# Epilogue of finished node blocks inside the edge loop of a graph attention layer on one Trainium2 core

## What is computed

```python
h_src, h_dst = x[src], x[dst]
e = leaky_relu(concat([h_src, h_dst, ef]) @ W_attn + b_attn)
m = concat([h_src, ef]) @ W_ne
ex = exp(e - segment_max(e, dst)[dst])
z = segment_sum(ex / segment_sum(ex, dst)[dst] * m, dst)
out = relu(concat([x, z]) @ W_out)
return layernorm(x + out)
```

## Time and profile before

| | us |
|---|---|
| median of 3 runs | 4009.47 (4005.22 to 4010.96) |
| profiled execution, its time | 4021.12 |
| profiled execution, span of its trace | 4019.2 |
| busy: POOL, DVE, PE, ACT | 2972.2, 2837.8, 2260.2, 2020.9 |

### The profile page before, as it was taken

The page is one execution under the profiler, slowest core; times in us unless marked ns, Lnnn a source line. Parts: engine busy times, 40 slices in busy tenths (PEclk is TensorE's granted clock), DMA queues, the critical chain, the costliest instruction groups (busy, mean ns, idle before and its releaser), DMA issues.

```text
span 4019.2 us, 47762 instructions
## 1 busy us (share of the span) xinstructions
PE 2260.2 (56%) x9822; PEld 2005.2 (50%) x9823; DVE 2837.8 (71%) x5649; ACT 2020.9 (50%) x3433; POOL 2972.2 (74%) x3133
## 2 busy tenths in 40 slices
PE   2666655555555555555555555555555555555556
PEld 1555555544454444454444444544444544454456
DVE  8776666666766767676676766676767676766777
ACT  2665555544454444444444444444444444444446
POOL 7777777777777777777777777777777777777770
PEclk9665556556556565555655555555655556555557
DMA  6655555555555555555555555555555555555542
GB/s 166 177 173 156 159 157 156 160 158 157 158 157 157 157 157 157 157 157 157 158 157 157 157 157 157 157 158 157 157 157 157 157 157 158 157 157 157 158 147 66
DMA packets 409354, 627.14 MB, mean 156 GB/s; under 512 B 208412, under 2 KB 208796, under 8 KB 409332
## 3 DMA queue, kind: packets, MB, share of 16 engines
q1 hardware_dynamic: 296260, 519.51, 40.7%
q0 software_dynamic: 100000, 102.60, 12.3%
q10 hardware_dynamic: 13072, 4.80, 0.6%
HBM read 621.58 MB, written 4.81 MB: 156 GB/s over the span
## 4 chain that ended last, share of the span: by engine, by line
POOL 73%; issue 24%; DVE 1%; PE 1%; POOLq 1%; ACT 0%; DMA 0%; DVEq 0%
POOL V L372 73%; POOLq L390 0%; PE psE L909 0%; POOLq L381 0%; PE psT L902 0%; PE psG L844 0%; DVE y L801 0%; DVE var L782 0%; DMA V<-in_x_dram,srcs 0%; DVE y L778 0%; DVE mean L791 0%; DVE y L798 0%; DVE prod L785 0%; DMA srcs<-in_src_dram 0%; ACT zb L522 0%
## 5 line engine op out<-in xcount | busy, mean ns | idle before, releaser
L372 POOL DMA_INDIRECT V<-in_x_dram,srcs x3125 | 2971.2, 951 | 956.0 <-issue 952.9
L844 PE MATMUL psG<-V,pT 128*128 128x130 f32 x6250 | 1461.4, 427 | 366.6 <-DVE psS L663 366.6
L844 PEld LDWEIGHTS psG<-V,pT 128*128 128x128 f32 x6250 | 1361.5, 330 | 506.1 <-DVE psS L663 506.1
L837 PE MATMUL psT<-ident,e 128*128 128x128 f32 x3125 | 720.8, 404 | 1286.3 <-DVE e L658 1286.3
L448 ACT COPY pT<-psT 128x512 f32<-128x512 f32 x784 | 420.9, 589 | 1714.8 <-PE psT L837 1708.9
L837 PEld LDWEIGHTS psT<-ident,e 128*128 128x128 f32 x3125 | 573.8, 215 | 1392.7 <-DVE e L658 1392.7
L594 DVE TENSOR_TENSOR prod<-V,psM 128x512 f32<-128x512 f32 x782 | 502.4, 684 | 637.6 <-DMA V<-in_x_dram,srcs 621.8
L658 DVE TENSOR_TENSOR e<-zb,psE 128x1024 f32<-128x1024 f32 x392 | 478.8, 1221 | 259.4 <-DVE u L599 162.1
L705 DVE CUSTOM_DVE_ANT_0 um<-ubc,psS 128x1024 f32<-128x1024 f32 x391 | 477.6, 1221 | 20.2 <-ACT psS L461 19.3
L599 DVE TENSOR_REDUCE u<-prod 128x8 f32<-128x1024 f32 x391 | 477.0, 1220 | 13.5
L469 ACT ACTIVATE psE<-um,ebias 128x1024 f32<-128x1024 f32 x391 | 437.2, 1118 | 12.8
(11 more groups left out here) (97 smaller groups left out, 524.7 us busy)
## 6 DMA issues: line engine op xcount, KB each, us to landing
ubc<-scores SPq DMA_DIRECT2D x391, 512.0 KB
dbc<-in_dst_dram SPq DMA_DIRECT2D x390, 512.0 KB, 4.0
V<-in_edge_attr_dram SPq DMA_DIRECT2D x390, 256.0 KB, 2.8
V<-in_x_dram,srcs POOLq DMA_INDIRECT x3125
srcs<-in_src_dram SPq DMA_DIRECT2D x390, 4.0 KB
scores<-u SPq DMA_DIRECT2D x390, 4.0 KB
out_dram<-y SPq DMA_DIRECT2D x12, 256.0 KB
xt<-in_x_dram ACTq DMA_DIRECT2D x6, 448.0 KB, 14.2
```

What stands on the lines that cost most here:

```text
L372: nc.gpsimd.indirect_dma_start(Vx[:, s, j, 1:XW], None, x[:, :], bass.IndirectOffsetOnAxis(ap=srcs[:, s, j:j + 1], axis=0)).then_inc(h_in[ ...
L837: last = nc.tensor.transpose(psT[:, i, (j - 4 * i) * P:(j - 4 * i + 1) * P], e1[:, 0:n * P].rearrange("q (p j) -> q j p", j=n)[:, j, :], i ...
L844: last = nc.tensor.matmul(psG[:, 0:AW], pT[:, i, (j - 4 * i) * P:(j - 4 * i + 1) * P], V[:, LEADIN + s * SLOT + XW * j:LEADIN + s * SLOT + ...
```

## The change

The loop now finishes one block in every second supertile of turns 7 to 38: 160 times. In an odd supertile DVE divides a block's sums by its denominator (`prepare`), PE turns the result, ACT copies it; two supertiles on, PE multiplies it with `wz`, and in the even supertile after that DVE does the rest for a block (`finish_one`). Each five blocks share one square root on ACT at the end of the turn and one scaling on DVE in the next (`scale_group`); SP stores five blocks in the turn after. Which block is finished where is computed on the chip once behind turn 6 (`tabulate`): a block may be finished once no later supertile touches it, at most one new block for each of the 160 places; where none is new, the last one is finished and stored again. By the reference's inputs the table runs from block 0 to block 94. The last supertile runs through the windows from `ends[0]` to the last block (by these inputs one window, block 97) and finishes one block in each of them, in a longer form of the window; the last six blocks are finished together behind the last merge.

```diff
+            def store_rows(k, q):
+                m = k - YT - 2
+                at = sp.snap(blocks[q], min_val=0, max_val=NB - 3)
+                sp.wait_ge(rows_out[q - 1], 16 * (m + 3) if q else 16 * (m + 2))
+                sp.wait_ge(scaled, m + 2)
+                sp.dma_start(out[bass.ds(at * P, P), :], ro[:, q, :]).then_inc(rows_out[q], 16)
...
+            finished(TURNS + 1)
+            for q in range(GROUP):
+                store_rows(TURNS + 1, q)
+            for q in range(GROUP):
+                sp.wait_ge(rows_out[q], 16 * (TURNS - YT) + 32)
+            sp.wait_ge(back_rows, 1)
...
+                    if not ahead:
+                        act.wait_ge(z_turned, late)
+                        nc.scalar.copy(zTs[:, :], zT_ps).then_inc(z_copied, 1)
+                        act.wait_ge(scaled, late_rows)
+                        rows = act.snap(of_block, min_val=0, max_val=NB - 3)
+                        act.dma_start(out[bass.ds(rows * P, P), :], ro[:, GROUP - 1, :]).then_inc(late_out, 16)
...
+                    if not ahead:
...
+                        act.wait_ge(fin_q, late)
+                        nc.scalar.activation(fs[:, GROUP - 1:GROUP], fv[:, GROUP - 1:GROUP], ACT.Sqrt).then_inc(std_ready, 1)
...
+                    if s % 2:
+                        act.wait_ge(z_turned, GROUP * (k - YT) + s // 2 + 2)
+                        nc.scalar.copy(zTs[:, :], zT_ps).then_inc(z_copied, 1)
+                act.wait_ge(fin_q, GROUP * (k - YT) + GROUP + 1)
+                nc.scalar.activation(fs[:, 0:GROUP], fv[:, 0:GROUP], ACT.Sqrt).then_inc(std_ready, 1)
+            act.wait_ge(z_done, EVENTS + 1)
...
+            act.wait_ge(rows_out[GROUP - 1], 16 * (TURNS - YT) + 32)
             supertile(TURNS, 0, False)
...
+            def prepare(f):
+                b = bass.ds(f, 1)
+                dve.wait_ge(z_turned, fp)
+                dve.wait_ge(rescaled, settled)
+                nc.vector.tensor_scalar(fl[:, 0:1], accv[:, b, 0], TINY, None, ALU.max).then_inc(fin_l, 1)
+                dve.wait_ge(fin_l, fp)
+                nc.vector.reciprocal(fl[:, 0:1], fl[:, 0:1]).then_inc(fin_rl, 1)
+                dve.wait_ge(fin_rl, fp)
+                nc.vector.tensor_scalar(zs[:, :], accv[:, b, 1:1 + 2 * F].rearrange("p b f -> p (b f)"), fl[:, 0:1], None, ALU.mult).then_inc(zs_ready, 1)
+                dve.reg_add(fp, fp, 1)
+
+            def finish_block(f, q, product):
+                b = bass.ds(f, 1)
+                dve.wait_ge(z_done, product)
+                nc.vector.tensor_tensor(fy[:, 0:F], z_out, y0[:, b, :].rearrange("p b f -> p (b f)"), ALU.add).then_inc(fin_y, 1)
+                dve.wait_ge(fin_y, fe)
+                nc.vector.scalar_tensor_tensor(fr[:, 0:F], fy[:, 0:F], 0.0, xt[:, b, :].rearrange("p b f -> p (b f)"), ALU.max, ALU.add).then_inc(fin_r, 1)
+                dve.wait_ge(fin_r, fe)
+                nc.vector.tensor_reduce(fm[:, 0:1], fr[:, 0:F], AX, ALU.add).then_inc(fin_m, 1)
...
+                nc.vector.scalar_tensor_tensor(fout[:, q, :], fm[:, 0:1].broadcast_to((P, F)), -1.0 / F, fr[:, 0:F], ALU.mult, ALU.add).then_inc(fin_c, 1)
...
+                nc.vector.tensor_tensor(fy[:, 0:F], fout[:, q, :], fout[:, q, :], ALU.mult).then_inc(fin_s, 1)
...
+                nc.vector.tensor_reduce(fv[:, q:q + 1], fy[:, 0:F], AX, ALU.add).then_inc(fin_w, 1)
...
+                nc.vector.tensor_scalar(fv[:, q:q + 1], fv[:, q:q + 1], 1.0 / F, EPS, ALU.mult, ALU.add).then_inc(fin_q, 1)
...
+            def scale(q, n):
+                nc.vector.reciprocal(rs[:, q:q + n], fs[:, q:q + n]).then_inc(rs_ready, 1)
+                dve.wait_ge(rs_ready, fd)
+                nc.vector.tensor_tensor(ro[:, q:q + n, :], fout[:, q:q + n, :], rs[:, q:q + n].unsqueeze(2).broadcast_to((P, n, F)), ALU.mult).then_inc(scaled, 1)
...
+            def scale_group(k):
+                dve.wait_ge(std_ready, k - YT + 1)
+                for q in range(GROUP):
+                    dve.wait_ge(rows_out[q], 16 * (k - YT + 1))
+                scale(0, GROUP)
...
+                if finishing and s == 0:
+                    scale_group(k)
+                if finishing and s % 2 == 0:
+                    finish_one(k, s // 2)
+                if finishing and s % 2 == 1:
+                    prepare(dve.snap(finish[s // 2 + 2], min_val=0, max_val=NB - 3))
                 if left >= 2:
...
+            tabulate()
...
+                finished(k)
...
+            dve.sem_inc(prod_done, 1)
+            dve.wait_ge(y_copied, PAIRS + 2)
+            scale_group(TURNS)
...
+            dve.wait_ge(rows_out[GROUP - 1], 16 * (TURNS - YT) + 32)
...
             supertile(TURNS, 0, 0)
...
+            def z_step(k, q):
+                pe.wait_ge(prod_done, RING * k + 2 * q + 4)
+                pe.wait_ge(z_copied, GROUP * (k - YT) + q + 1)
+                z_multiply().then_inc(z_done, 1)
+                pe.wait_ge(zs_ready, GROUP * (k - YT) + q + 1)
+                z_turn().then_inc(z_turned, 1)
...
+                    if not ahead:
+                        pe.wait_ge(zs_ready, late)
+                        z_turn().then_inc(z_turned, 1)
+                        pe.reg_add(late, late, 1)
+                        pe.wait_ge(z_copied, late)
+                        z_multiply().then_inc(z_done, 1)
                     window(s, J if ahead else JL)
```

More of the change, by code:

```diff
@@ L321, in _, with finished @@
                 load_src(RING + s, s)
-            with sp.Fori(1, TURNS - 1) as k:
+            blocks = [sp.alloc_register(f"block_sp{q}") for q in range(GROUP)]
+            def finished(k):
+                at = GROUP * (k - YT - 2)
+                sp.load(blocks, fint[0:1, bass.ds(at, GROUP)] if not isinstance(k, int) else fint[0:1, at:at + GROUP])
+            def store_rows(k, q):
[4 more added lines that the diff above has]
+                sp.dma_start(out[bass.ds(at * P, P), :], ro[:, q, :]).then_inc(rows_out[q], 16)
+            with sp.Fori(1, YT + 2) as k:
                 for s in range(RING):
                     step(k, s)
+            sp.wait_ge(table, 1)
+            with sp.Fori(YT + 2, TURNS - 1) as k:
+                finished(k)
+                for s in range(RING):
+                    step(k, s)
+                    if 0 < s <= GROUP:
+                        store_rows(k, s - 1)
+            finished(TURNS - 1)
             for s in range(RING):
@@ L329, in _ @@
                 step(TURNS - 1, s)
+                if 0 < s <= GROUP:
+                    store_rows(TURNS - 1, s - 1)
+            finished(TURNS)
             for s in range(RING - LEAD):
@@ L499, in _ @@
             weights_out(1)
[L502 to L526, removed]
-                    nc.scalar.activation(ubc[:, par, 0:w2 * F].rearrange("p (b f) -> p b f", f=F), y0[:, bass.ds(8 * (o - 2), w2), :],
-                                         ACT.Square).then_inc(sq_ready, 1)
-            octets(octet, 3)
+            act.wait_ge(scaled, late_rows)
+            rows = act.snap(of_block, min_val=0, max_val=NB - 3)
+            act.dma_start(out[bass.ds(rows * P, P), :], ro[:, GROUP - 1, :]).then_inc(late_out, 16)
+            act.reg_add(sent, sent, 16)
+            act.wait_ge(back_turned, 1)
+            nc.scalar.copy(pT[:, 0, :], psT[:, 0, :])
+            nc.scalar.copy(pT[:, 1, 0:(BACK - 4) * P], psT[:, 1, 0:(BACK - 4) * P]).then_inc(back_copied, 1)
+            act.wait_ge(late_out, sent)
+            act.wait_ge(back_var, 1)
+            nc.scalar.activation(fs[:, :], fv[:, :], ACT.Sqrt).then_inc(back_std, 1)
         @block.vector
@@ L682, in pass_on @@
                 dve.reg_add(g, g, 1)
-            def supertile(k, s, left, y_steps=None):
+            fe = dve.alloc_register("finishing")
+            fp = dve.alloc_register("preparing")
+            finish = [dve.alloc_register(f"finish{q}") for q in range(GROUP + 2)]
+            dve.reg_mov(fe, 1)
+            dve.reg_mov(fp, 1)
+            settled = dve.alloc_register("settled")
+            fd = dve.alloc_register("scaling")
+            dve.reg_mov(fd, 1)
+            def prepare(f):
[8 more added lines that the diff above has]
+                dve.reg_add(fp, fp, 1)
@@ L685, in supertile @@
+            def supertile(k, s, left, y_steps=None, finishing=False):
                 t = RING * k + s
@@ L693, in supertile @@
                     ts = bass.ds(t, 1)
+                    if left == 0:
+                        prepare(dve.snap(of_block, min_val=0, max_val=LAST - 1))
+                        scale_late()
                     weigh()
@@ L805, in _ @@
+            nc.vector.tensor_scalar(fv[:, :], fv[:, :], 1.0 / F, EPS, ALU.mult, ALU.add).then_inc(back_var, 1)
+            dve.wait_ge(back_std, 1)
+            step(nc.vector.reciprocal(rs[:, :], fs[:, :]))
+            nc.vector.tensor_tensor(rows, rows, spread(rs), ALU.mult).then_inc(back_rows, 1)
         @block.tensor
```

270 lines of the change are left out of this document (174 added, 96 removed).

## The result

| | before | after |
|---|---|---|
| median, four runs each | 4009.43 us (4005.22 to 4010.96) | 4122.01 us (4121.49 to 4122.65) |
| ratio, 95% interval | | 1.0283 (1.0265 to 1.0300) |
| span of the profiled execution | 4019.2 us | 4119.9 us |

The forecast was 3994, the range ended at 4046. The change costs 112.6 us.

A forecast was written before the change was run, and what follows sets the result against it. POOL's gathers were taken to bound the loop, hiding 14.7 of DVE's 14.85 us added per turn. The end's -27.7 us and DVE's lag of 12.8 gave -14.9, from the median 4009.47 to 3994; range 3979 to 4046.

The forecast's parts named there:

- the start of a turn: DVE at each turn's beginning: seven more registers and a possible wait for ACT, 1.1 us more, bounds 0 to 2.
- the sum: All work added to DVE in a turn: 14.85 us against 14.7 free, with bounds of 12 to 18.
- finish_block: DVE's work for one block: six operations of 64 columns, a small one and gaps, 1.82 us.
- odd supertiles behind ACT's copy: In odd supertiles L459 and L461 queue behind ACT's copy of the turned block; just fits, cost 0, bound 0.7 each.
- scaling to the last window: five stores: At the end ACT and DVE wait for five stores, each waiting for the one before: 8.75 us, 7 to 11.5.
- last window, L730 to L730: In the last window PE turns the block only behind its eight matmuls: 12.4 us instead of 6.33.
- last merge to the end: Behind the last merge six blocks are finished together, from matmuls to stores: 13.8 us.
- the free time: DVE's waits for gathers in a turn, 17.1 us less nine gaps of 0.27: 14.7 us to hide new work in.
- the tail: The end of the span behind the last gathers: 3991.5 against 4019.2, so -27.7 us without DVE's lag, bounds 5 each way.
- DVE becomes the bound: In each turn's ten blocks, DVE work beyond 14.7 us costs 32 us per microsecond; at 1.9 over, 4050; chance 0.28.
- The pair is held for the whole operation: DVE's new operations hold up POOL's gathers for their whole length: POOL loses 17 us, time 4001; chance 0.05.
- A pause behind each table load: ACT's switches between exponential and root each pause as long as the load: 82 us beyond the forecast, 4076; chance 0.03.

## Why the prediction was wrong

**The step that failed is the start of a turn**, 1.1 us with bounds 0 and 2. It priced seven registers, and a jump back that costs what it cost before. The jump back did not stay what it was: 0.25 us in before, 3.07 in after. With the load's 1.63 that is 4.45 more, and the start measured 4.5 more instead of 1.1; besides, two operations in the turn come 0.4 late. No row of before shows such a fetch, for before never had one: the bounds were taken from rows in which the resource is not used up. The body's length, which was there to be counted, did not enter the sum, and neither did the load's own record in before: 1.37 us for twenty registers, more than the 1.1 taken for seven.

The Trainium skill has the mechanism, "Runtime: NRT & Kernel Launch", section "Instruction fetch mechanics": an engine's instruction store holds two blocks of 256 instructions, and a taken branch to a block outside of it waits for a fetch. The runs agree with the wait, and not with two blocks as what stays: the body from 104 to 478 lies in two such blocks and was fetched anew each turn. Whether the store is smaller, or keeps room for a line ahead, no run shows. By that section of the Trainium skill a load takes about 0.2 us a register, by estimate 1.4 for seven and 4 for twenty; the traces do not bear that out, with 1.63 for seven and 1.37 for twenty.

**Of the rest, term by term:**

| term | predicted | measured |
|---|---|---|
| `finish_block` | 1.82 | 1.81, and 0.4 late once a turn |
| `prepare` | 0.78 | 0.75, and 0.4 late once a turn |
| `scale_group` | 0.75 | 0.70 |
| start of a turn, more than before | 1.1 (0 to 2) | 4.5; 1.6 without the fetch |
| odd supertiles behind ACT's copy | 0 | nothing new: 14.6 us of waits for L513 in the whole span, 19.3 for L461 before |
| `tabulate`, once | 8 | 7.4 |
| scaling to the last window: five stores | 8.75 | 8.4 |
| last window, L730 to L730 | 12.4 | 12.55 |
| last merge to the end | 13.8 | 13.8 |

The operations, down to 64 columns that no row showed, came out within a tenth. So did the free time: without the fetch the sum is 13.0 + 0.75 + 1.6 = 15.35, 0.65 over the 14.7, and the ten turns from 2500 on measured 0.4 longer than before (100.79 against 100.42). Over all 32 turns, from the loop's first L730 to the third last of the span, it is 3216.9 against 3197.5, 0.6 a turn. The working has one slip: the steps up to the five stores add up to 3947.5, not 3947.7, which changes nothing.

**Two smaller errors are in the 8.7 us that are left without the fetch.** The load of registers was 0.5 too small: 32 turns make 16 us. And the tail was set against a profiled execution that was itself slow in the tail. The same epilogue, in the kernel with the load added to before and used, from its last merge on (columns as in the earlier trace rows):

```profile
3943.50:4004.10 60.60, 35.49 (x294) 33.08 (x294) 50.44 (x108) 42.91 (x150) 0.00 (x0) 0.88 0.21 54
```

The 294 matmul records take 35.5 us here and 44.8 in the earlier trace rows; the mean granted clock is 0.88 here and 0.73 there, both between the two levels of 1.2 and 2.4 GHz. From the third last `weigh` (L658 in before) to the end of the span this kernel takes 78.2 us, not 83.2. Of the five traces that have this tail, two take 83.2 (before, and the loop at 239), at a mean granted clock of 0.72, and three take 78.0 to 78.2, at 0.78 to 0.85; the two long ones are also the longest executions. So against most executions the tail wins 23, not 28: part of the 11.65 us between profiled execution and median lay in the very piece that the change removes, and was counted twice; that the tail came out as forecast is in part luck. Why some executions were granted less is open. With the first block of the loop, for which DVE waits 2.4 us once, -15 + 16 + 5 + 2.4 = +8.4; measured +8.7, which is closer than the terms are known. The fetch adds the other 104.

**The rivals.** "DVE becomes the bound" named the right engine and the right price, 32 us for each microsecond of a turn, but its worst case was 1.9 over; the turn became 4.0 longer, by a cause that it did not name. "The pair is held for the whole operation" did not show: the gathers take 946 to 950 ns in all kernels with the change, and 948 to 951 in the five without it, where the rival's 17 us would have made them 5 ns longer. By the rule of the Trainium skill, "SBUF — State Buffer", section "SBUF: two separate sides", which it states for a GpSimd operation that reads SBUF, they would have become longer; no run shows it. "A pause behind each table load" did not show either. ACT's timeline at the start of a turn of the changed kernel:

```profile
2720.92 1.28 ACT L565 ACT_TABLE_LOAD   x1
2722.21 0.21 ACT L565 ACTIVATE fs<-fv 128x5 f32<-128x5 f32 x1
2723.61 1.28 ACT L508 ACT_TABLE_LOAD   x1 [1.19 <-issue]
2724.91 0.29 ACT L508 ACTIVATE nbias<-nidbias,wshift 128x1 f32 x1
```

Both directions of the switch cost the load alone; the next operation starts 0.01 to 0.02 behind it, and the 1.19 ahead of the second load stand there without a load too (1.35 ahead of an L459 of before). By the Trainium skill, "ScalarE: Activation LUTs", section "What ACT_TABLE_LOAD costs", each would be 2.66; the trace shows 1.28.

What the prediction said of ACT, that DVE would wait about 1 us for it if the registers cost nothing, turned out right in kind (2.4 in the kernel with the loads early): it was the next wait, hidden as long as DVE was later itself.

## What to carry to other kernels

When a loop body grows, count its instructions and see which fetch lines it lies in, before any of its operations is priced; the instruction queue of the page tells at once whether a loop is being fetched again. A bound that comes from rows of before holds only for resources that the change does not use up. And a saving is to be set against an execution that was ordinary in the piece that is saved.

## What the runs showed of the hardware

- A DVE loop of 374 instructions stays in the store when it lies in three lines of 128 (start at 0 or at 130, 19 and 20 packets), and is fetched anew each turn in four (at 104 and 150, 170 packets); 303 instructions in four lines are fetched too (167). Each turn then costs 5 packets of 8,192 bytes, 2.5 to 2.9 us at the jump back, and with the 374 instructions two or three stalls of 0.37 at borders of lines.
- A load of seven registers costs DVE 1.6 to 1.9 us at the start of a turn, and 0.6 when it is issued behind a product of 1.28 us. The load's own record takes 1.63 us for seven registers and 1.37 for twenty.
- The root's table load and the load back took 1.28 us each, with no pause behind them (0.01 and 0.02).
